# First layer's running states: sixteen chained products per sequence become seven single ones, added up in SBUF by GpSimd

## The chip, the cores and the metric

One core of one Trainium2 chip runs the whole program. The metric is the device time of one execution in microseconds; less is better. The kernel before was timed three times.

## What is computed

Four transformer layers follow each other on an input of 8 sequences of 512 tokens with 128 features. The change touches the attention of the first layer alone. Cut to what matters:

```python
def _L0_attn_ref(x, W1, b1, W2, b2):          # 16 heads of 8 features
    k, q, v = jnp.split(x @ W1 + b1, 3, axis=-1)
    mask = jnp.tril(jnp.ones((t, t), dtype=bool))
    attn = jnp.where(mask, jnp.einsum('bhqd,bhkd->bhqk', q, k), 0.0)
    out = jnp.einsum('bhqk,bhkd->bhqd', attn, v)
    return out @ W2 + b2
# x = x + _L0_attn_ref(_layernorm(x), ...), then a mixture of experts, then three more layers
```

There is no softmax, so the sum over earlier keys can be split. The 512 tokens are cut into 8 chunks of 64. Within a chunk the scores are made and masked. For all earlier chunks, q is multiplied with a state: the sum of k (outer) v over all tokens before the chunk, a 128x128 matrix of which the 16 diagonal blocks of 8x8 are kept. Chunks 1 to 7 need a state each.

## The kernel before

Each engine has its own program, and semaphores order them. For the first layer `STEPS0` gives every piece of work of a sequence b a due time on each engine that takes part, and `lanes` sorts the pieces of all 8 sequences by these times with 7.53 between sequences. The result, `ORDER0`, is one fixed list per engine. Each engine works its list strictly in order; a piece that waits holds up all behind it. The pieces are these: `l0a_s`/`l0a_n` are the normalisation (statistics on DVE, the inverse root by POOL's `rstd`, the scaling on DVE, transposes on PE, a copy by ACT), `l0_q` and `l0_kv` the projections, `l0_sc0` and `l0_sc1` the scores of chunks 0 to 3 and 4 to 7 with their masking on DVE, `l0_st` the states, `l0_o` the output, `l0_pj` the projection and the addition to X, `l0f_s`/`l0f_n` the second normalisation, and `l0t_*` the routing of the tokens. The last of these, `l0t_x`, is four indirect DMAs on POOL (line 2126).

I call the stretch from one `l0_st` to the next a step. In a middle step PE's list is (b is the sequence whose states are made)

    st.b  t_r.(b-2)  l0a_n.(b+2)  kv.(b+1)  sc0.(b+1)  o.b  t_c.(b-2)  l0f_n.(b-1)  pj.b  q.(b+2)  sc1.(b+1)

and DVE's is

    sc1.b  l0a_s.(b+3)  st.b  t_r.(b-2)  t_m.(b-2)  l0a_n.(b+3)  kv.(b+1)  sc0.(b+1)  l0f_n.(b-1)  t_w t_c t_i.(b-2)  pj.b  l0f_s.b

POOL's is `l0a_s.(b+3) l0a_n.(b+1) t_x.(b-3 or so) l0f_s.b`: for sequence 3, for instance, `t_x.0 f_s.2 a_s.6 a_n.4`.

`l0_st` on PE makes the seven states in one PSUM unit of two banks. State c (1 to 7) is the sum over the c // 2 whole tiles of 128 tokens before it, and half a tile (64 tokens) if c is odd. Each is summed in PSUM by a chain of products: 12 products over 128 rows (line 706) and 4 over 64 rows (line 708), 16 in all; whole and half products take turns. Every float32 product appears in the trace as two matrix instructions. DVE then multiplies the 896 columns by the head mask on their way to SBUF (line 1523, tile `l0_S`, which the trace calls K). `l0_o` waits for that and for the masked scores, then multiplies each state with q (line 738) and the scores with v (line 744). A ring of four PSUM units is shared by all pieces of the first layer (`unit`, `filled`, `drained`); a piece may fill its unit when the piece four units earlier has been drained.

Of the kernel before, what the change touches and what calls it, by code (L numbers as in the profile page):

```python
# [11 lines left out]
ALU = mybir.AluOpType  # L12
# [3 lines left out]
B, T, D, H, HD = 8, 512, 128, 16, 8  # L16
# [60 lines left out]
def lanes(pieces, gap):  # L77
# [18 lines left out]
    ("l0_st", dict(PE=21.86, DVE=22.8)),  # L96
# [240 lines left out]
def count_units():  # L337

    out, at, uses = {}, {3: 0, 4: 0}, [0] * 4
    for name, b in FILL:  # L340
        ring = 4 if name[:2] == "l0" else 3
        for k in range(UNITS.get(name, 0)):
# [13 lines left out]
         "logits_on", "hot", "tsub", "texp", "slots", "scatter0", "scatter1", "y0_in", "y1_in", "mixed",  # L356
# [8 lines left out]
def build(nc, inp, out):  # L365
    with ExitStack() as ctx:
# [99 lines left out]
        def drained_of(key, k=0):  # L466
            return drained[UNIT[key[0], key[1], k][0]]
# [20 lines left out]
        l0_S = [kflat[i][:, 512:1408].rearrange("p (c d) -> p c d", c=7) for i in range(2)]  # L488
        l0_oT = [tmpA[:, 1024 + 512 * i:1536 + 512 * i] for i in range(2)]
# [94 lines left out]
        def pe_program(e):  # L584
# [96 lines left out]
            for name, b in ORDER0["PE"]:  # L681
# [16 lines left out]
                elif name == "l0_st":  # L698
# [3 lines left out]
                    for c in range(1, 8):  # L702
                        t, half = divmod(c, 2)
                        o = p[:, 128 * (c - 1):128 * c]
                        for tt in range(t):
                            m = PE.matmul(o, ktok[i][:, tt, :], v_dense(i, tt, 0, 128), start=(tt == 0), stop=(tt == t - 1 and not half))
                        if half:
                            m = PE.matmul(o, ktok[i][0:64, t, :], v_dense(i, t, 0, 64), start=(t == 0), stop=True)
# [18 lines left out]
                elif name == "l0_o":  # L727
                    u, n, p = unit((name, b))
                    e.wait_ge(drained_of(("l0_st", b)), after(("l0_st", b)))
# [5 lines left out]
                    for t in range(4):  # L735
                        for c in range(2):
                            if 2 * t + c:
                                PE.matmul(p[:, 512 * c + 64 * t:512 * c + 64 * t + 64], l0_S[i][:, 2 * t + c - 1, :],
                                          qf[i][:, 128 * t + 64 * c:128 * t + 64 * c + 64], start=True, stop=False, skip_group_check=True)
# [374 lines left out]
        def dve_program(e):  # L1114
# [369 lines left out]
            for name, b in ORDER0["DVE"]:  # L1484
# [33 lines left out]
                elif name == "l0_st":  # L1518
                    u, n, p = unit((name, b))
                    if b > 1:  # L1520
# [3 lines left out]
                                    in0=p[:, 0:896].rearrange("p (c h e) -> p c h e", c=7, h=H),  # L1524
# [529 lines left out]
        def pool_program(e):  # L2054
# [81 lines left out]
            for name, b in ORDER0["POOL"]:  # L2136
                if name in ("l0a_s", "l0f_s"):
                    if (name, b) != ("l0a_s", 0):
                        rstd((name, b))
                elif name == "l0a_n":  # L2140
                    add_bias(("l0a_n", b), "l0_b2")
                elif name == "l0t_x":
                    scatter(0, b)
# [353 lines left out]
```

## Time and profile before

| what | value |
|---|---|
| time, median of 3 | 1372.38 us (1365.06, 1372.38, 1373.85) |
| span of the profiled execution | 1367.5 us |
| PE busy over the whole span | 1136.0 us, 83% |
| DVE busy | 824.0 us, 60% |
| ACT busy | 568.1 us, 42% |
| POOL busy | 447.1 us, 33% |
| the first layer's attention and routing | about 8 to 200 us of the span |

The span is the time from the first to the last instruction of one execution, and busy time is the time in which an engine has an instruction under way. A product on PE shows twice, as a weight load (PEld) and as the matrix pass (PE). The profiled execution is one of the faster: 4.9 us below the median.

### The profile page before, as it was taken

To read this page: it belongs to the slowest core of one execution; us is meant where nothing else is said; L and a number is where in the kernel's file an instruction comes from. 1 tells how busy PE (TensorE), PEld (TensorE's weight loads), DVE (VectorE), ACT (ScalarE), POOL (GpSimd) and SP (SyncE) were. 2 spreads that over 40 slices of the span, in tenths; PEclk is the share of its full clock that TensorE was granted. 3 is DMA by queue.
4 is the path that set the end of the run, shared out by engine and by line. 5 is a ranking of instruction groups with operands and counts; after the bars stand their busy time and mean duration, and the time that the engine had idled before them with its cause. 6 is when DMAs were issued, how large, how long until landed. Compare 5 with 4: busy or idle time off the path is not lost.

```text
span 1367.5 us, 39578 instructions
## 1 busy us (share of the span) xinstructions
PE 1136.0 (83%) x16979; PEld 814.2 (60%) x16979; DVE 824.0 (60%) x2399; ACT 568.1 (42%) x993; POOL 447.1 (33%) x538
## 2 busy tenths in 40 slices
PE   6999968888976798687888988888898887987895
PEld 4677747777764374444555655656565564654784
DVE  7587764568885122356858587686848675644432
ACT  3322102455452131314373754737375462542332
POOL 3123331344564144113122313233321302112575
PEclk9999979999986899899999999999999998999998
DMA  9355415533140421222211211212221110201784
GB/s 364 150 206 204 179 63 180 170 126 120 35 157 22 114 59 48 51 57 54 55 50 53 65 50 41 63 43 59 59 59 50 41 32 11 56 11 45 192 208 89
DMA packets 85169, 126.18 MB, mean 92 GB/s; under 512 B 14465, under 2 KB 66178, under 8 KB 84578
## 3 DMA queue, kind: packets, MB, share of 16 engines
q1 hardware_dynamic: 68258, 106.57, 24.6%
q0 software_dynamic: 10928, 13.64, 4.2%
q10 hardware_dynamic: 5808, 3.43, 1.0%
q8 instruction: 134, 2.20, 0.7%
q14 instruction: 41, 0.34, 0.1%
HBM read 50.92 MB, written 46.74 MB: 71 GB/s over the span
## 4 chain that ended last, share of the span: by engine, by line
PE 36%; DVE 25%; issue 16%; ACT 10%; POOL 6%; DMA 5%; SPq 2%; another core or an unknown queue 0%; ACTq 0%; DVEq 0%; POOLq 0%
DVE mx L1705 9%; ACT MW L1988 4%; DVE bst L1137 2%; PE ps L994 2%; PE ps L782 2%; PE ps L783 2%; DVE mx L1696 2%; PE ps L1058 2%; PE ps L795 1%; PE ps L985 1%; DVE X L1165 1%; POOL xs L2126 1%; PE ps L1089 1%; PE ps L907 1%; POOL rst L2072 1%
## 5 line engine op out<-in xcount | busy, mean ns | idle before, releaser
L1705 DVE TENSOR_REDUCE mx<-ps 128x2 f32<-128x1024 f32 (+3 forms) x176 | 188.7, 1121 | 30.2 <-PE ps L1026 30.0
L1988 ACT ACTIVATE MW<-ps 128x1024 f32<-128x1024 f32 x160 | 154.8, 1030 | 74.7 <-PE ps L1043 62.2
L2126 POOL DMA_INDIRECT xs<-xr,sidu x96 | 96.0, 1000 | 132.6 <-DVE sidu L1296 96.3
L2069 POOL TENSOR_SCALAR rst<-bmv 128x4 f32<-128x4 f32 x64 | 15.9, 248 | 288.0 <-DVE bmv L1140 287.4
L1058 PE MATMUL ps<-MW,Vp 128*16 128x128 f32 x2560 | 87.3, 277 | 4.7 <-ACT MW L1988 4.4
L1026 PE MATMUL ps<-K,Q 64*128 64x512 bf16 (+3 forms) x512 | 60.0, 303 | 18.7 <-DVE mx L1705 11.5
L1975 ACT ACTIVATE MW<-ps 128x1024 f32<-128x1024 f32 x64 | 63.4, 1027 | 27.5 <-PE ps L956 25.7
L1058 PEld LDWEIGHTS ps<-MW,Vp 128*16 128x16 f32 x2560 | 63.8, 97 | 16.1 <-ACT MW L1988 5.7
L2152 POOL DMA_INDIRECT out_dram<-qf,toku x39 | 60.7, 1555 | 35.3 <-DVE toku L1761 26.2
L1794 ACT COPY XT<-ps 128x512 f32<-128x512 f32 x48 | 28.2, 587 | 102.2 <-PE ps L616 85.7
L1696 DVE TENSOR_REDUCE mx<-ps 128x8 f32<-128x768 f32 x64 | 58.1, 950 | 16.6 <-PE ps L933 14.5
L1043 PE MATMUL ps<-Q,K 64*128 64x128 bf16 x1280 | 58.2, 221 | 5.6 <-DVE mx L1696 2.2
L2048 ACT ACTIVATE MW<-ps,MW 128x256 f32<-128x256 f32 (+1 forms) x92 | 34.0, 440 | 60.5 <-PE ps L1103 58.4
L616 PE MATMUL ps<-W,xr 128*128 128x128 f32 x192 | 33.8, 304 | 27.9 <-DVE xr L1150 16.5
L2152 POOL DMA_INDIRECT ys<-xp,toku x38 | 38.0, 1000 | 56.4 <-DVE toku L1549 47.6
L1137 DVE BATCH_NORM_STATS2 bst<-X 128x6 f32<-128x128 f32 x256 | 55.4, 279 | 1.2
L1043 PEld LDWEIGHTS ps<-Q,K 64*128 64x128 bf16 x1280 | 38.5, 95 | 27.3 <-issue 12.9
L2072 POOL TENSOR_TENSOR rst<-rst,npow 128x4 f32<-128x4 f32 x48 | 49.9, 1039 | 4.0
L782 PE MATMUL ps<-tco,MW 128*128 128x256 f32 x152 | 46.9, 391 | 3.7 <-ACT tco L1864 1.3
L1026 PEld LDWEIGHTS ps<-K,Q 64*128 64x128 bf16 x512 | 18.6, 94 | 50.9 <-DVE mx L1705 17.0
L649 PE MATMUL ps<-W,tmpA 128*128 128x128 f32 x256 | 40.5, 286 | 10.1 <-ACT MW L1988 4.1
L1165 DVE TENSOR_TENSOR X<-ps,X 128x512 f32<-128x512 f32 x40 | 27.6, 690 | 35.2 <-PE ps L754 11.5
(379 smaller groups left out, 2713.0 us busy)
## 6 DMA issues: line engine op xcount, KB each, us to landing
xs<-hb SPq DMA_DIRECT2D x52, 528.0 KB, 9.2
MW<-l_moe_dram SPq DMA_DIRECT2D x19, 768.0 KB
MW<-l_moe_dram SPq DMA_DIRECT2D x20, 578.0 KB
Q<-spl SPq DMA_DIRECT2D x48, 128.0 KB
Q<-spm SPq DMA_DIRECT2D x48, 128.0 KB
K<-spl SPq DMA_DIRECT2D x43, 128.0 KB
K<-spm SPq DMA_DIRECT2D x43, 128.0 KB
MW<-l_moe_dram SPq DMA_DIRECT2D x16, 256.0 KB
```

The costliest lines, as they stand in the source:

```text
L782: PE.matmul(p[:, 256 * jj:256 * jj + 256], wt_[:, 128 * j:128 * j + 128], xsT0[s % 2], start=True, stop=True)
L1026: m = PE.matmul(p[:, o:o + nk], Q3[i][64 * k:64 * k + 64, s, 128 * t:nk], K3[i][64 * k:64 * k + 64, s, 0:nk], start=True, stop=True, tile_ ...
L1043: m = PE.matmul(p[:, o:o + 128], K3[i][64 * k:64 * k + 64, 4 * half + s, 128 * kt:128 * kt + 128], Q3[i][64 * k:64 * k + 64, 4 * half + s, ...
L1058: m = PE.matmul(ps[32 * j:32 * j + 16, 7, 128 * g:128 * g + 128], Vp[1][:, 4 * i + kt, h, :], P3[k % 2][:, col(h)[0] + 128 * col(h)[1]:col ...
L1137: own.end(V.bn_stats(out=bst[:, k, t, :], in_=X[:, 4 * b + t, :]))
L1696: V.tensor_reduce(out=mx[0][:, :, 4 * half:4 * half + 4, t], in_=p.rearrange("p (e n) -> p e n", e=2)[:, :, 0:384].rearrange("p e (s k) -> ...
L1705: V.tensor_reduce(out=mx[1][:, :, s0:s0 + ns, t], in_=p.rearrange("p (e n) -> p e n", e=2)[:, :, 0:ns * nk].rearrange("p e (s k) -> p e s ...
L1975: A.activation(P2[t % 2][:, 1024 * half:1024 * half + 1024], p, ACT.Exp).then_inc(drained[u], 1)
L1988: A.activation(P3[k % 2][:, 1024 * half:1024 * half + 1024], p, ACT.Exp).then_inc(drained[u], 1)
L2072: G.tensor_tensor(out=rst[:, k, 1, :], in0=rst[:, k, 0, :], in1=npow[:, :], op=ALU.pow).then_inc(rstd_on[k], 1)
L2126: G.indirect_dma_start(out=xs[L], out_offset=bass.IndirectOffsetOnAxis(ap=sidu[:, 4 * b + t:4 * b + t + 1], axis=0), in_=src[:, t, :], in_ ...
L2152: G.indirect_dma_start(out=dst, out_offset=at, in_=y[:, v, :], in_offset=None, compute_op=how).then_inc(y_out[k], 16)
```

## The change

PE makes seven independent products per sequence: one for each of the three whole tiles and one for the first half of each of the four tiles. DVE masks them into SBUF as before. GpSimd (POOL) then adds: whole[1] += whole[0], whole[2] += whole[1], each 128x128, and half[1:4] += whole[0:3], 128x384; each addition waits for the one before. `l0_o` waits for a new semaphore, `states`, that the last addition raises, in place of DVE's drain. The tile holds the states in another order (three whole ones, then four odd ones), and `state_at` finds them. Since `l0_st` now has a due time of 33.0 on POOL, POOL's list becomes, for sequence 3, `t_x.0 f_s.2 st.3 a_s.6 a_n.4`: the additions stand before `l0a_s.(b+3)`.

```diff
-    ("l0_st", dict(PE=21.86, DVE=22.8)),
+    ("l0_st", dict(PE=21.86, DVE=22.8, POOL=33.0)),
...
+        def state_at(c):
+            return c // 2 - 1 if c % 2 == 0 else 3 + c // 2
...
-                    for c in range(1, 8):
-                        t, half = divmod(c, 2)
-                        o = p[:, 128 * (c - 1):128 * c]
-                        for tt in range(t):
-                            m = PE.matmul(o, ktok[i][:, tt, :], v_dense(i, tt, 0, 128), start=(tt == 0), stop=(tt == t - 1 and not half))
-                        if half:
-                            m = PE.matmul(o, ktok[i][0:64, t, :], v_dense(i, t, 0, 64), start=(t == 0), stop=True)
+                    for t in range(3):
+                        PE.matmul(p[:, 128 + 128 * t:256 + 128 * t], ktok[i][:, t, :], v_dense(i, t, 0, 128), start=True, stop=True)
+                    for t in range(4):
+                        m = PE.matmul(p[:, 512 + 128 * t:640 + 128 * t], ktok[i][0:64, t, :], v_dense(i, t, 0, 64), start=True, stop=True)
                     m.then_inc(filled[u], 1)
...
                 elif name == "l0_o":
-                    e.wait_ge(drained_of(("l0_st", b)), after(("l0_st", b)))
+                    e.wait_ge(sem["states"], b + 1)
...
-                                PE.matmul(..., l0_S[i][:, 2 * t + c - 1, :],
+                                PE.matmul(..., l0_S[i][:, state_at(2 * t + c), :],
...
-                                    in0=p[:, 0:896].rearrange("p (c h e) -> p c h e", c=7, h=H),
+                                    in0=p[:, 128:1024].rearrange("p (c h e) -> p c h e", c=7, h=H),
...
+                elif name == "l0_st":
+                    i, key = b % 2, ("l0_st", b)
+                    whole, half = l0_S[i][:, 0:3, :], l0_S[i][:, 3:7, :]
+                    e.wait_ge(drained_of(key), after(key))
+                    own.end(G.tensor_tensor(out=whole[:, 1, :], in0=whole[:, 1, :], in1=whole[:, 0, :], op=ALU.add))
+                    e.wait_ge(own.sem, own.now)
+                    own.end(G.tensor_tensor(out=whole[:, 2, :], in0=whole[:, 2, :], in1=whole[:, 1, :], op=ALU.add))
+                    e.wait_ge(own.sem, own.now)
+                    G.tensor_tensor(out=half[:, 1:4, :], in0=half[:, 1:4, :], in1=whole, op=ALU.add).then_inc(sem["states"], 1)
```

## Rows read from the trace of the kernel before

**Rows 1.** Busy time in a stretch: length, PE, PEld, DVE, ACT, POOL busy (xcount), PEclk, DMA, GB/s.
```profile
80.00:100.00 20.00, 19.48 (x409) 15.19 (x409) 15.73 (x58) 5.95 (x10) 7.77 (x9) 1.00 0.52 202
```

**Rows 2.** Timeline of PE, step 3: start us, us, what, xcount, idle before.
```profile
81.85 1.12 PE L722 MATMUL ps<-Q,K 32*64 32x256 f32 x32
82.90 0.49 PE L708 MATMUL ps<-Vp,tmpA 64*128 64x128 f32 x2
83.31 0.71 PE L706 MATMUL ps<-Vp,tmpA 128*128 128x128 f32 x4
83.95 0.48 PE L708 MATMUL ps<-Vp,tmpA 64*128 64x128 f32 x2
...
85.87 1.60 PE L706 MATMUL ps<-Vp,tmpA 128*128 128x128 f32 x12
87.41 0.49 PE L708 MATMUL ps<-Vp,tmpA 64*128 64x128 f32 x2
87.82 1.06 PE L631 MATMUL ps<-W,XT 128*128 128x12 f32 x8
...
92.08 0.43 PE L738 MATMUL ps<-qf,K 128*128 128x64 f32 x2
```

**Rows 3.** Timeline of DVE, step 3 and the next steps' first masks, same columns.
```profile
85.35 2.36 DVE L1516 TENSOR_TENSOR MW<-ps,W 128x1024 f32<-128x1024 f32 x2 [3.03 <-remote]
...
88.82 1.06 DVE L1523 TENSOR_TENSOR K<-ps,W 128x896 f32<-128x896 f32 x1
...
90.57 0.87 DVE L1188 TENSOR_TENSOR spm<-spm 128x16 f32<-128x16 f32 x1
...
91.98 1.11 DVE L1150 TENSOR_SCALAR xr<-X,bmv,rst 128x128 f32<-128x128 f32 x4
...
96.66 1.10 DVE L1150 TENSOR_SCALAR xr<-X,bmv,rst 128x128 f32<-128x128 f32 x4
...
101.25 0.69 DVE L1165 TENSOR_TENSOR X<-ps,X 128x512 f32<-128x512 f32 x1
...
105.87 1.23 DVE L1516 TENSOR_TENSOR MW<-ps,W 128x1024 f32<-128x1024 f32 x1 [2.61 <-remote]
...
126.01 2.36 DVE L1516 TENSOR_TENSOR MW<-ps,W 128x1024 f32<-128x1024 f32 x2 [1.91 <-remote]
...
146.75 2.36 DVE L1516 TENSOR_TENSOR MW<-ps,W 128x1024 f32<-128x1024 f32 x2 [3.93 <-remote]
...
163.73 2.36 DVE L1516 TENSOR_TENSOR MW<-ps,W 128x1024 f32<-128x1024 f32 x2 [1.06 <-remote]
```

**Rows 4.** Timeline of DVE, steps 1 and 2, same columns.
```profile
43.79 2.36 DVE L1516 TENSOR_TENSOR MW<-ps,W 128x1024 f32<-128x1024 f32 x2 [1.34 <-PE ps L722]
...
63.00 2.36 DVE L1516 TENSOR_TENSOR MW<-ps,W 128x1024 f32<-128x1024 f32 x2 [0.72 <-PE ps L722]
```

**Rows 5.** Timeline of POOL, step 3, same columns.
```profile
80.37 1.23 POOL L2126 DMA_INDIRECT xs<-xr,sidu  x1 [11.32 <-DVE sidu L1296]
...
84.45 0.96 POOL L2126 DMA_INDIRECT xs<-xr,sidu  x1 [0.30 <-issue]
...
89.31 1.04 POOL L2072 TENSOR_TENSOR rst<-rst,npow 128x4 f32<-128x4 f32 x1
90.32 1.09 POOL L2083 TENSOR_TENSOR X<-X,W 128x512 f32<-128x512 f32 x1
```

**Rows 6.** POOL's instructions grouped by line and form: xcount, busy us, mean ns.
```profile
L2189 POOL TENSOR_TENSOR rr<-rr,rt 128x512 f32<-128x512 f32 x16 | 20.5, 1279 | 75.4 <-DVE rt L1661 75.4
L2113 POOL TENSOR_TENSOR mx<-mx,msp 128x64 f32<-128x64 f32 x16 | 4.9, 308 | 1.3
```

**Rows 7.** Busy time in a stretch at half clock and the one before it, columns as in Rows 1.
```profile
34.60:38.00 3.40, 1.89 (x98) 1.41 (x85) 0.00 (x0) 0.38 (x1) 0.00 (x0) 1.00 0.03 9
38.00:41.40 3.40, 3.14 (x10) 2.54 (x11) 0.93 (x3) 0.20 (x1) 0.00 (x0) 0.50 0.46 188
```

**Rows 8.** Timeline of PE at the end of the states, last sequence.
```profile
167.96 0.43 PE L738 MATMUL ps<-qf,K 128*128 128x64 f32 x2 [0.44 <-DVE K L1523]
```

More of the change, by code:

```diff
@@ L355 @@
          "pv0", "pv1", "og_out0", "og_out1",
-         "logits_on", "hot", "tsub", "texp", "slots", "scatter0", "scatter1", "y0_in", "y1_in", "mixed",
+         "logits_on", "hot", "states", "tsub", "texp", "slots", "scatter0", "scatter1", "y0_in", "y1_in", "mixed",
          "tab", "pattern", "g_half", "gx0", "gx1", "gx2", "gx3", "gw0", "gw1", "gw2", "gw3", "turned", "gT", "g_act", "g_down", "g_y", "g_tok",
@@ L737, in pe_program @@
                             if 2 * t + c:
-                                PE.matmul(p[:, 512 * c + 64 * t:512 * c + 64 * t + 64], l0_S[i][:, 2 * t + c - 1, :],
+                                PE.matmul(p[:, 512 * c + 64 * t:512 * c + 64 * t + 64], l0_S[i][:, state_at(2 * t + c), :],
                                           qf[i][:, 128 * t + 64 * c:128 * t + 64 * c + 64], start=True, stop=False, skip_group_check=True)
```

## Prediction

> **What bounds the kernel now.** I first looked for the place of the change in the timeline of PE. The states of sequence 3 take PE from 82.90 to 87.82, 4.92 us, and the row below each run shows where it ends [rows 2]. The busy time per stretch then says whether PE is what the first layer waits for: 19.48 of 20 us busy at full clock, DVE 15.73, POOL 7.77 [rows 1]. PE is the bound of this stage, and time taken from it should be time won, eight times. That is the tempting answer. The rest of the reading asks what comes second, and how far behind.
>
> For that I followed one step on DVE and POOL. X is the moment at which PE's last score product of a step ends, s the moment at which DVE starts the first mask of these scores. In step 3, X is 81.85 + 1.12 = 82.97 [rows 2] and s is 85.35 [rows 3]: DVE had waited 3.03 us, and the trace has no instruction as the releaser ("remote"). In steps 1 and 2, s (43.79 and 63.00) comes 0.1 us after the product [rows 4]. What is new from step 3 on is POOL's series of four indirect DMAs, 80.37 to 85.41 [rows 5]; all five steps that have it show the wait [rows 3]. So a mask signal seems to arrive 2 to 3 us late while POOL issues these DMAs. I take this as it stands; the cause is not in the rows.
>
> From s, DVE runs without a gap that matters: masks and statistics to the state mask at 88.82 = s + 3.5, its end at s + 4.5, routing, scaling of sequence b+3 at 91.98 = s + 6.6, the second norm's scaling at 96.66 = s + 11.3, the addition to X at 101.25 = s + 15.9 and statistics to s + 17.9 [rows 3]. A step takes 20.5 us (85.35 to 105.87). DVE is thus only 2.6 us behind PE, less than what the change takes from PE.
>
> **What PE gives up.** A run of 12 instructions lasts 85.87 to 87.41, 1.54 us, one of 4 lasts 83.31 to 83.95, 0.64 us [rows 2]: 0.11 us an instruction and 0.20 us for each turn between whole and half products. Before: 32 x 0.11 + 7 x 0.20 = 4.92, as the trace has it. After: 7 products are 14 instructions, 1.54 us, and 2 turns, 0.40: 1.95 us. PE gives up 3.0 us per sequence, 24 us in all.
>
> **What POOL adds.** The trace has no addition of this size on POOL. Below lies 128x64 at 308 ns, above 128x512 at 1279 ns [rows 6] or 1090 ns [rows 5]. On the line through 308 and 1090 (1.75 ns a column) 128 columns take 0.42 and 384 take 0.87 us: 2 x 0.42 + 0.87 + three handovers of 0.07 to 0.1 = 1.95 us, which I round to 2.0 with the first wait. The ends are 3 x 0.31 = 0.9 and 3 x 1.28 = 3.8 us. I take the line, since both sizes lie inside it.
>
> POOL's own page bears on this. The Trainium skill (GPSIMD Engine Reference, section 3.1) gives an addition on GpSimd about 2.6 cycles per element at 1.2 GHz. By that estimate 640 columns would be 1.4 us plus dispatch; the rows and the page agree within what the ends leave open.
>
> Then I place the additions. They need DVE's state mask, whose end is s + 4.55, so the states are ready at s + 6.65, where the old `l0_o` needed only s + 4.55. In steps 0 to 4 the inverse root for sequence b+3 (1.04 us [rows 5] and 0.3 for the short instruction before it, 1.35 us) now queues behind them on POOL: ready at s + 8.0 where it was ready at s + 5.0. DVE needs it at s + 6.6 and stands 1.4 us; everything behind it on DVE (kv, score masks, second norm) moves by that. The second norm's scaling ends at s + 13.8, and PE's transposes wait for it. Where no sequence b+3 exists (steps 5 to 7) this does not arise.
>
> One more thing is shared. The routing addition of 128x16 on DVE took 0.87 us at 90.57 [rows 3], while POOL's big addition ran from 90.32 to 91.41 [rows 5]; it ended with it. So DVE operations with two SBUF inputs stand still while POOL adds. Three such operations follow the state mask. In steps 3 and 4 they fall into the 1.4 us that DVE loses anyway; in steps 5 and 6 they may cost DVE up to 1 us, which is covered, since PE needs the norm only at s + 11.5 and DVE has it at s + 10.2.
>
> The Trainium skill states this as a rule (SBUF — State Buffer, section "SBUF: two separate sides"): the port pair of VectorE and GpSimd is an exclusive lock. It speaks against work on GpSimd; here it would add at most 2 steps x 1 us if the cover were gone, 2 us to the sum.
>
> **Step by step.** Old PE from X to `l0_o`: 92.08 - 82.97 = 9.1 us, 8.2 in steps 0 and 1, which have no routing product (0.9) [rows 2].
>
> - Step 0: PE could start `l0_o` at X + 5.3, the states come at X + 0.1 + 6.7 = X + 6.8. Gain 1.5, and PE stands 1.5.
> - Step 1: `l0_o` at s + 6.7, its end s + 12.3 (5.6 us without the fetch gap in it), norm at s + 13.8, then transposes, projection, q and scores 0.5 + 0.9 + 1.8 + 1.05: X' = s + 18.2. It was 19.2 (43.79 to 63.00 [rows 4]): gain 0.9.
> - Step 2 likewise, then the late signal (2.4 to 3 us): 20.8 against 22.35 (63.00 to 85.35): 1.5.
> - Steps 3 and 4: X' = s + 18.1, DVE ready at s + 19.3, signal at s + 20.8, against 20.5 and 20.1 [rows 3]: lost 0.3 and 0.7. DVE starts POOL's next DMAs at s + 17.4, so X' again falls inside them.
> - Step 5: no b+3. States at s + 5.4, X' = s + 16.2, signal s + 19.3, against 20.7: gain 1.4. Step 6, without q: X' = s + 13.95 and signal s + 16.1, against 17.0: gain 0.9.
> - Step 7: the states come at s + 5.5, PE started `l0_o` at 167.96 = s + 4.2 [rows 8]: lost 1.2.
>
> Sum: 1.5 + 0.9 + 1.5 - 0.3 - 0.7 + 1.4 + 0.9 - 1.2 = 4.0 us gained out of 24. The rest of PE's 24 us turns into standing before `l0_o` and before the second norm, some 3 us per step.
>
> **The clock.** The granted clock was 0.50 from 38.0 to 41.4, that is the level of 1.2 GHz, after PE had been busy for only 1.89 of the 3.40 us before [rows 7], and such a stretch costs half its length, 1.7 us. New standing of 1.5 us twice a step invites more of them. I allow one more than before: 4.0 - 1.7 = 2.3 us. The profiled span of 1367.5 becomes 1365.2. The median of the runs stands 4.9 us above that span, so I predict 1370.1 us. Later stages get the same instructions in the same order and I move nothing there.
>
> **The rivals.**
>
> A. PE's time counts in full: 24 us, 1348 us. For it speaks the 97% of PE [rows 1]. It needs states at X + 6.2, while even with s = X + 0.1 they come at X + 6.8. Chance 0.06.
>
> B. The signal is no longer late, because X' and the DMAs part. Then steps 2 to 6 run at DVE's s + 19.3 or PE's X': up to 1.5 to 2 us more each, 8 us in all: 1362 us. Chance 0.12.
>
> C. POOL's additions cost as much as its dearest row, 1.28 us each [rows 6]. 3.84 us in place of 1.95, 1.9 us more in each of 8 steps, 15 us: 1385 us, slower. It passes the old time once the three additions exceed 1.95 + 2.3 / 8 = 2.2 us, and is slower by 1% from about 4 us. Against it, a quarter of the columns at a quarter of the row's price is the pattern of the rows. Chance 0.10.
>
> D. The clock drops in every step: 8 x 1.7 = 13.6 in place of 1.7, so 1382 us. For it speaks standing of 3 us per step; against it, PE has about 1 us of cover in steps 1 to 4. Chance 0.10. The Trainium skill (TensorE: Matmul & The Clock Gate, Part 1) says that idle time returns PE to the half rate; the trace agrees at 38.0.
>
> My own case holds 0.62.
>
> **How the numbers follow.** A measurement of this kernel can tell about 1%, 13.7 us, from no change. The range runs from B's 1362 less 3 for the spread of the runs (1365 to 1374) up to D's 1382: 1359 to 1382 us. It leaves out A (0.06) and most of C (0.10). A lies below 1358.7, and of B a few hundredths may; above 1386.1 lie half of C, by the spread of the runs, and little of D. Faster 0.08, same 0.84, slower 0.08.
>
> **What would show it.** PE's states take 1.95 us (14 instructions). POOL shows three additions of about 0.42, 0.42 and 0.87 us per sequence. PE stands 1.5 us before line 738 with POOL as the releaser, and before line 616 with DVE's scaling. DVE's line 1150 waits about 1.4 us for POOL's inverse root in steps 0 to 4. PE's busy time falls by 24 us, the span hardly. The end of the first layer comes 2 to 4 us earlier. I am wrong if the additions are far from 2 us, if s is no longer 2 to 3 us behind X, or if stretches at 1.2 GHz appear in most steps.

## The result, and the profile after

| kernel | median | runs | ratio to before, 95% interval | profiled span |
|---|---|---|---|---|
| before | 1372.43 us (1365.06 to 1375.33) | 15 | | 1367.5 us |
| after | 1382.31 us (1373.72 to 1391.70) | 15 | 1.0072 [1.0051, 1.0094] | 1375.3 us |

The change makes the kernel 0.7% slower: less than 1%, but clear of zero, and to the other side of the small gain I had worked out. The predicted 1370.1 us is 12 us too low, and 1382.3 lies just above the range. The same text gave 1.0040 [1.0018, 1.0062], 1.0039 [1.0013, 1.0065] and 1.0072 [1.0046, 1.0097] in three further comparisons, each on another chip.

The first layer's end can be read in both traces, from the mark that POOL sets after the last indirect DMA. The first line is before, timeline of POOL (start, us, what):

```profile
199.40 0.10 POOL L2062 MEMSET mark<- 128x1 f32 x1 [1.42 <-DMA xs<-xr,sidu]
```

and this is after, same view:

```profile
209.58 0.10 POOL L2064 MEMSET mark<- 128x1 f32 x1 [1.44 <-DMA xs<-xr,sidu]
```

So the first layer ends 10.2 us later, and the span grows by 7.8; the rest of the program took 2.4 us less in this execution. All that follows is about these 10.2 us. With s as in the prediction (start of DVE's first mask of a step), the steps of both kernels in us are:

| step | 0 | 1 | 2 | 3 | 4 | 5 | 6 | last s to the mark |
|---|---|---|---|---|---|---|---|---|
| before | 21.0 | 19.2 | 22.3 | 20.5 | 20.1 | 20.7 | 17.0 | 35.7 |
| after | 21.4 | 20.8 | 22.8 | 21.3 | 21.3 | 20.6 | 17.5 | 40.8 |
| predicted change | -1.5 | -0.9 | -1.5 | +0.3 | +0.7 | -1.4 | -0.9 | +1.2 |
| measured change | +0.4 | +1.5 | +0.4 | +0.8 | +1.2 | -0.1 | +0.5 | +5.1 |

(The first s is 0.3 us later as well.) Every step misses by 0.5 to 2.4 us, the tail by 3.9.

After, timeline of PE, step 3; it answers to [rows 2]. The field in brackets is the idle time before the row and what ended it:

```profile
85.84 0.94 PE L708 MATMUL ps<-Vp,tmpA 128*128 128x128 f32 x6
86.71 1.16 PE L710 MATMUL ps<-Vp,tmpA 64*128 64x128 f32 x8
88.89 1.06 PE L636 MATMUL ps<-W,XT 128*128 128x12 f32 x8 [1.03 <-ACT K L1847]
89.81 0.63 PE L621 MATMUL ps<-W,xr 128*128 128x128 f32 x4
90.41 3.37 PE L701 MATMUL ps<-W,XT 128*128 128x256 f32 x8
...
95.00 0.43 PE L740 MATMUL ps<-qf,K 128*128 128x64 f32 x2
...
102.75 0.63 PE L621 MATMUL ps<-W,xr 128*128 128x128 f32 x4 [1.12 <-DVE xr L1152]
```

The states take 85.84 to 87.87, 2.0 us, as worked out. But two things follow that the sum did not have. PE stands 1.03 us for ACT's copy of q (it holds the PSUM unit that the next piece wants; before, the 4.92 us of products covered it). And the k and v products of line 701 take 3.37 us, in a stretch of half clock (1.89 us in e8_gap_fill below, at the full one).

After, timeline of DVE, step 3; it answers to [rows 3]:

```profile
88.00 2.35 DVE L1518 TENSOR_TENSOR MW<-ps,W 128x1024 f32<-128x1024 f32 x2 [2.71 <-remote]
...
91.47 1.06 DVE L1525 TENSOR_TENSOR K<-ps,W 128x896 f32<-128x896 f32 x1
...
96.12 1.80 DVE L1152 TENSOR_SCALAR xr<-X,bmv,rst 128x128 f32<-128x128 f32 x4 [1.39 <-POOL rst L2074]
...
101.50 1.10 DVE L1152 TENSOR_SCALAR xr<-X,bmv,rst 128x128 f32<-128x128 f32 x4
...
109.30 1.22 DVE L1518 TENSOR_TENSOR MW<-ps,W 128x1024 f32<-128x1024 f32 x1 [1.22 <-remote]
```

After, timeline of POOL, step 3; it answers to [rows 5]:

```profile
89.09 1.05 POOL L2074 TENSOR_TENSOR rst<-rst,npow 128x4 f32<-128x4 f32 x1
92.61 0.46 POOL L2148 TENSOR_TENSOR K<-K 128x128 f32<-128x128 f32 x1 [2.47 <-DVE K L1525]
93.14 0.45 POOL L2150 TENSOR_TENSOR K<-K 128x128 f32<-128x128 f32 x1
93.67 1.02 POOL L2152 TENSOR_TENSOR K<-K 128x384 f32<-128x384 f32 x1
94.67 0.22 POOL L2071 TENSOR_SCALAR rst<-bmv 128x4 f32<-128x4 f32 x1
94.97 1.04 POOL L2074 TENSOR_TENSOR rst<-rst,npow 128x4 f32<-128x4 f32 x1
95.98 1.09 POOL L2085 TENSOR_TENSOR X<-X,W 128x512 f32<-128x512 f32 x1
```

The three additions take 92.61 to 94.69, 2.1 us. The inverse root waits behind them and is ready at 96.01 = s + 8.0, and DVE stands 1.39 us for it: all of this as predicted. New is the length of DVE's scaling at 96.12. It takes 1.80 us where [rows 3] has 1.11, because POOL's addition of the bias (95.98 to 97.07) now runs beside it. In the kernel before, that addition met the small routing operation instead (0.87 us in [rows 3]). Now that operation takes 0.40 us beside POOL's first additions, and a later one (line 1196) 0.66 us, both within the time that DVE loses anyway. The second norm is therefore ready at 102.60 = s + 14.6, not s + 13.8.

After, busy time in stretches, columns as in [rows 1], to be laid beside [rows 1] and [rows 7]:

```profile
60.10:63.50 3.40, 3.40 (x10) 1.78 (x8) 1.94 (x9) 0.32 (x1) 0.22 (x1) 0.51 0.78 318
172.80:206.90 34.10, 23.29 (x320) 18.70 (x321) 20.82 (x119) 2.48 (x6) 14.50 (x16) 0.50 0.06 21
80.00:100.00 20.00, 18.21 (x319) 13.27 (x320) 14.74 (x57) 5.35 (x9) 9.65 (x12) 0.83 0.45 179
```

The granted clock is at the level of 1.2 GHz once in every step (36.3 for 6.8 us, then 60.1, 80.6, 90.9, 111.3, 131.8 and 152.3 for 3.4 us each), where before had it at 38.0 only. At the end it stays there for 34.1 us (before 17.1, from 178.0). In the stretch 80 to 100 PE is busy for 18.21 us in place of 19.48, at a mean clock of 0.83 in place of 1.00. Over the whole span it is busy for 1129.3 us in place of 1136.0: 6.7 us less and not 24, while its mean granted clock falls from 0.946 to 0.931. The prediction's last sign of being wrong, stretches at 1.2 GHz in most steps, is there.

After, timeline of PE in the last sequence; it answers to [rows 8]:

```profile
175.10 0.69 PE L740 MATMUL ps<-qf,K 128*128 128x64 f32 x2 [5.55 <-POOL K L2152]
175.72 1.19 PE L746 MATMUL ps<-MW,Vp 64*32 64x64 f32 x64
176.84 1.11 PE L740 MATMUL ps<-qf,K 128*128 128x64 f32 x4
```

PE stands 5.55 us where it stood 0.44, and then works at half the clock (1.11 us for four instructions, 0.66 at the full one).

### The profile page after: what moved, and what is told of

Its sections match the earlier page's. It is cut to its first block, busy times and chain, and to the rows that moved or that the text cites. A ratio compares the mean times of both kernels' runs of the same rounds, so it can differ in the third digit from the quotient of the medians.

```text
span 1375.3 us, 39322 instructions
## 1 busy us (share of the span) xinstructions
PE 1129.3 (82%) x16835; PEld 809.6 (59%) x16835; DVE 829.9 (60%) x2399; ACT 567.6 (41%) x993; POOL 461.6 (34%) x562
## 3 DMA queue, kind: packets, MB, share of 16 engines
q1 hardware_dynamic: 68258, 106.57, 24.4%
## 4 chain that ended last, share of the span: by engine, by line
PE 36%; DVE 27%; issue 14%; ACT 9%; POOL 5%; DMA 4%; SPq 1%; another core or an unknown queue 1%; PEldq 1%; ACTq 0%; DVEq 0%; PEld 0%; POOLq 0%
DVE mx L1707 9%; ACT MW L1990 4%; DVE bst L1139 2%; PE ps L996 2%; DVE MW L1518 2%; PE ps L1105 2%; PE ps L1091 2%; PE ps L784 2%; PE ps L1060 2%; PE ps L785 1%; PE ps L797 1%; PE ps L987 1%; DVE X L1167 1%; DVE mx L1698 1%; DVE xr L1152 1%
## 5 line engine op out<-in xcount | busy, mean ns | idle before, releaser
L1028 PE MATMUL ps<-K,Q 64*128 64x512 bf16 (+3 forms) x512 | 60.5, 305 | 17.8 <-DVE mx L1707 10.3
L1698 DVE TENSOR_REDUCE mx<-ps 128x8 f32<-128x768 f32 x64 | 58.0, 949 | 16.7 <-PE ps L935 14.6
L1152 DVE TENSOR_SCALAR xr<-X,bmv,rst 128x128 f32<-128x128 f32 x128 | 39.6, 370 | 29.4 <-POOL rst L2074 27.8
L621 PEld LDWEIGHTS ps<-W,xr 128*128 128x128 f32 x192 | 24.2, 159 | 43.3 <-issue 20.6
L654 PE MATMUL ps<-W,tmpA 128*128 128x128 f32 x256 | 40.4, 285 | 10.2 <-ACT MW L1990 4.1
```

The lines of the kernel that those rows point to most:

```text
L621: m = PE.transpose(p[:, 128 * t:128 * t + 128], xr_of(key)[:, t, 0:128], ident)
L1028: m = PE.matmul(p[:, o:o + nk], Q3[i][64 * k:64 * k + 64, s, 128 * t:nk], K3[i][64 * k:64 * k + 64, s, 0:nk], start=True, stop=True, tile_ ...
L1698: V.tensor_reduce(out=mx[0][:, :, 4 * half:4 * half + 4, t], in_=p.rearrange("p (e n) -> p e n", e=2)[:, :, 0:384].rearrange("p e (s k) -> ...
```

## The experiments

The theories before the first run: **order** (the inverse root behind the additions on POOL delays DVE, and PE's second norm with it), **clock** (the half-clock stretches cost what their length says), **tail** (the last sequence alone), **additions** (their 2 us are on the path), and as their rival that **PE's relief** is worth something which something else eats. Steps are given as in the table above. "Before" beside a run is the kernel before on the same chip.

### Undoing one part each

**e1_no_additions**: the seven products without the additions (the states are then incomplete); `l0_o` waits for DVE's drain.

```diff
-                    e.wait_ge(sem["states"], b + 1)
+                    e.wait_ge(drained_of(("l0_st", b)), after(("l0_st", b)))
```

> The changed kernel with the three GpSimd additions left out (the later chunks' states are then incomplete); the output products wait for DVE's mask as before. This is what the shorter product work is worth when the sum is free. Theory 1 (the way over GpSimd is what costs: additions of 2 us before the output products, the inverse root behind them): the states are there at s + 4.6 instead of s + 6.6, no wait of DVE for the inverse root, a step of 18 to 18.5 us in place of 20.5 to 22.8, some 2 us won per step against the kernel before: 1355 to 1360 us. Theory 2 (PE's saved time can't be used at all, since DVE and the ring of PSUM units bind anyway): 1368 to 1374 us, no difference from before.

Measured: 0.9963 [0.9945, 0.9982] (before 1360.37). First layer's end 191.0 us. PE's relief alone is worth 0.37%, 5 us, of the 24 us that PE gives up. (Later stages work on other values here, since the states lack terms; that their time is unaffected by this is not shown.)

**e2_root_first**: the kernel after with one number changed, so that POOL's list is `t_x f_s a_s st a_n`, the inverse root ahead of the additions.

```diff
-    ("l0_st", dict(PE=21.86, DVE=22.8, POOL=33.0)),
+    ("l0_st", dict(PE=21.86, DVE=22.8, POOL=33.5)),
```

> The changed kernel with the due time of the additions on POOL at 33.5 in place of 33.0, so that the inverse root of sequence b+3 stands before the additions in POOL's list; everything else is the same. Theory 1a (the inverse root behind the additions is the larger part of the loss, by DVE and then by PE's transposes): DVE's waits for it (3.6, 3.6, 1.4, 1.4, 1.4 us) vanish, steps 1 to 4 are 1 to 1.5 us shorter: 1375 us. Theory 3 (the clock: PE's standing before the transposes is what lets it fall to 1.2 GHz in each step) expects in addition fewer half-clock stretches between 50 and 115 us, and 1370 to 1372 us. If neither holds the time stays at 1382.

Measured: 0.9998 [0.9973, 1.0022]. Steps 18.6 17.3 18.9 19.4 19.2 19.7 18.6, then 41.2, mark 196.2. The number undoes the loss, but gains nothing on the kernel before. Its median, 1358.49 us, is 3.4 us above e1's on the same chip: that is what the additions still cost with the root ahead of them.

**e7_additions_only**: the kernel before with its sixteen products, and three additions of the same sizes on POOL (`z` is a spare tile), whose results nobody needs; `l0_o` waits for them.

```diff
+                elif name == "l0_st":
+                    ...
+                    own.end(G.tensor_tensor(out=z[:, 0:128], in0=l0_S[i][:, 1, :], in1=l0_S[i][:, 0, :], op=ALU.add))
+                    ...
+                    G.tensor_tensor(out=z[:, 256:640], in0=kflat[i][:, 640:1024], in1=kflat[i][:, 1024:1408], op=ALU.add).then_inc(sem["states"], 1)
```

> The kernel before, with all its 16 products, but with three GpSimd additions of the same sizes into a spare tile, at the same place in GpSimd's list, and the output products waiting for them. It has the whole cost of the change and none of its relief. Where mask signals are in time, s = X + 0.1, the additions end at X + 6.8 and the output products start at X + 9.1 anyway, the norm is ready at X + 14.6 against 15.6: no loss but for the last sequence, 1.000 to 1.002. Where they are 2 to 3 us late the additions end at X + 9.3 and the norm is 1.5 us late: 1 to 2 us a step from step 3 on, 1.004 to 1.008. By the clock theory it is 1.000 on either chip, since PE hardly stands.

Measured: 1.0081 [1.0050, 1.0111] (before 1359.69); first layer's end 208.3. The additions with their wait cost 0.8%; with e1 (on another chip) that closes within the intervals: -0.4% for PE's relief, +0.8% for the additions, and +0.4% is what the kernel after shows on e7's chip. I had expected 1.000 to 1.002 for a chip without late mask signals, and this is one: that miss says that the cost needs no late signal. One view of e7, groups of DVE's instructions by line (the last field is the idle time before them and what ended it), shows where the cost enters, even with PE's old list:

```profile
L1150 DVE TENSOR_SCALAR xr<-X,bmv,rst 128x128 f32<-128x128 f32 x52 | 17.8, 401 | 13.2 <-POOL rst L2072 13.2
```

The same group before (on another chip; b1_before_trace and e4_before_grouped wait for the root as long, 3.2 us):

```profile
L1150 DVE TENSOR_SCALAR xr<-X,bmv,rst 128x128 f32<-128x128 f32 x52 | 14.4, 341 | 3.2 <-POOL rst L2072 3.2
```

DVE waits 10 us more for the inverse root and is 3.4 us longer busy with the scaling. (Both views run from 20 to 215 us. The 3.2 us of before lie after the last sequence's states; inside the steps it waits for no root, and e7 11.3 us: 3.57 in steps 0 and 1, 1.39 in each of 2 to 4.)

**e5_dve_additions**: the additions on DVE, right behind its mask; POOL's list as before.

> The changed kernel's seven products, with the three additions on DVE right behind its mask, and GpSimd's list as before the change. Theory 1 (what costs is the way over GpSimd): three DVE additions of about 0.3, 0.3 and 0.6 us with handovers, 1.3 us in place of 2.05, and no inverse root behind them: the states at s + 5.9, the norm on PE 1.3 us later than in the kernel before, 0.998 to 1.002 of it. Theory 2 (DVE is the next bound, so any time given to DVE is lost): DVE's own step grows to 19.2 us, and with PE at 17 to 18 the ratio is still 0.995 to 1.000. Above 1.003 both would be wrong.

Measured: 1.0018 [0.9990, 1.0046] (before 1369.66); steps 21.1 16.8 19.1 23.2 23.3 21.9 16.7, then 40.6. Its step 1, 16.8 us, is shorter than that of any other kernel that computes all the states; but the tail is as long as in the kernel after. So a long tail does not need POOL to do the additions; how much of it the wait for them makes is measured by e10 and e11 below.

### The kernel after, before and root-first on other chips

Here **a1_after_again**, **a2_after_third** and **a3_after_fourth** are the kernel after, **b0_before_again** and **b1_before_trace** the kernel before, **e2b_root_first** is e2's text.

> The kernel before, unchanged, on the chip of this group of runs, for its trace. The other chip's trace had mask signals 2 to 3 us late while GpSimd issued its DMAs; the traces of e1_no_additions to e4_before_grouped have none. If the lateness belongs to the chip or the execution and not to the kernel, it is absent here too, and a middle step takes 20.1 us by PE alone, as there; if it belongs to the length of the state products it is back.

> The changed kernel, unchanged, beside the others. e2_root_first came out at 0.9998 of the kernel before with one change of order; if the inverse root behind the additions is the cause of the loss, this one is again at 1.006 to 1.009. If it comes out at 1.000 too, the loss belonged to the first chip (late signals, clock), and the order has no part in it.

> The changed kernel, unchanged, for comparison with the other order on one chip: 1.004 to 1.007 of the kernel before, as on the two chips so far.

> The edit of e2_root_first again, now on the same chip as the changed kernel. If the inverse root behind the additions carries the loss, this stays at 1.000 +/- 0.002 while the changed kernel is at 1.004 or above. If the difference between the two was that of the chips, both have the same ratio.

> The kernel before, for a trace on the same chip as the other three. 1.000. If the late mask signals belong to the chip, all four kernels of this call show them or none does; if they belong to the kernel's timing, they may differ. The first layer's end without late signals is expected at 192 to 197 us, with them at 199 to 202 us.

> The kernel after once more, on the chip of e11. 1.004 to 1.007 as on the three chips before; tail 39 to 41.2 us, PE's stand in front of the last l0_o 4.8 to 5.6 us, clock at half from 166-173 us on for 34 us or in several stretches of as much together. Step 1 (no late signal on any chip) 20.7 to 20.8 us.

| label | ratio, 95% interval | steps | last s to the mark | mark |
|---|---|---|---|---|
| b0_before_again | 0.9989 [0.9965, 1.0014] | 19.0 19.3 22.4 21.4 20.5 20.1 17.9 | 37.8 | 201.5 |
| b1_before_trace | 1.0030 [1.0002, 1.0057] | 19.3 19.3 22.4 20.5 20.1 19.2 17.9 | 35.4 | 197.2 |
| a1_after_again | 1.0040 [1.0018, 1.0062] | 20.4 20.7 20.6 22.9 22.6 20.3 16.9 | 39.2 | 206.7 |
| a2_after_third | 1.0039 [1.0013, 1.0065] | 21.7 20.8 20.0 20.3 20.1 18.6 18.6 | 41.2 | 204.4 |
| a3_after_fourth | 1.0072 [1.0046, 1.0097] | 20.5 20.7 20.6 23.0 23.0 21.8 17.5 | 40.8 | 210.7 |
| e2b_root_first | 0.9995 [0.9969, 1.0021] | 18.6 17.3 19.2 19.2 19.3 18.0 18.6 | 41.2 | 194.6 |

The kernel before came out at 1.0030 against itself once. Differences of 0.3% between single comparisons are therefore not evidence; four comparisons of the kernel after, all above 1.0035, are. The mark is the sharper measure: 206.7 to 210.7 us (204.4 on a2's chip) against 197.2 to 201.5. On a2's chip, which has no late mask signals, the kernel before has no trace; what is compared with a2 there is e2b, 9.8 us earlier.

Step 1 repeats best, since no mask signal is late in it: 19.2 or 19.3 us in three traces of before, 20.7 or 20.8 in four of after, 17.3 in three of root-first (e2, e2b and, below, e10). Its rows show the order theory at work. DVE in step 1 of b1_before_trace:

```profile
42.38 2.36 DVE L1516 TENSOR_TENSOR MW<-ps,W 128x1024 f32<-128x1024 f32 x2 [0.72 <-PE ps L722]
47.27 1.09 DVE L1523 TENSOR_TENSOR K<-ps,W 128x896 f32<-128x896 f32 x1 [1.34 <-PE ps L708]
48.28 1.11 DVE L1150 TENSOR_SCALAR xr<-X,bmv,rst 128x128 f32<-128x128 f32 x4
...
53.25 1.11 DVE L1150 TENSOR_SCALAR xr<-X,bmv,rst 128x128 f32<-128x128 f32 x4
```

in a2_after_third:

```profile
44.76 2.36 DVE L1518 TENSOR_TENSOR MW<-ps,W 128x1024 f32<-128x1024 f32 x2 [2.38 <-PE ps L724]
48.23 1.05 DVE L1525 TENSOR_TENSOR K<-ps,W 128x896 f32<-128x896 f32 x1
52.85 1.81 DVE L1152 TENSOR_SCALAR xr<-X,bmv,rst 128x128 f32<-128x128 f32 x4 [3.57 <-POOL rst L2074]
...
58.24 1.09 DVE L1152 TENSOR_SCALAR xr<-X,bmv,rst 128x128 f32<-128x128 f32 x4
```

and in e2b_root_first:

```profile
41.69 2.36 DVE L1518 TENSOR_TENSOR MW<-ps,W 128x1024 f32<-128x1024 f32 x2 [0.73 <-PE ps L724]
45.15 1.06 DVE L1525 TENSOR_TENSOR K<-ps,W 128x896 f32<-128x896 f32 x1
46.78 3.06 DVE L1152 TENSOR_SCALAR xr<-X,bmv,rst 128x128 f32<-128x128 f32 x4 [0.57 <-POOL rst L2074]
...
53.42 1.10 DVE L1152 TENSOR_SCALAR xr<-X,bmv,rst 128x128 f32<-128x128 f32 x4
```

The second norm is ready at s + 12.0 before, s + 14.6 after, s + 12.8 with the root first. In steps 0 and 1 there is no routing work to fill the gap, so DVE stands 3.57 us for the root, not 1.4; I had read the wait off step 3. With the root first the wait is 0.57 us, but the scaling takes 3.06 us in place of 1.11. It now runs beside the additions themselves and the bias, timeline of POOL in e2b_root_first:

```profile
46.65 0.45 POOL L2148 TENSOR_TENSOR K<-K 128x128 f32<-128x128 f32 x1
47.18 0.46 POOL L2150 TENSOR_TENSOR K<-K 128x128 f32<-128x128 f32 x1
47.72 0.99 POOL L2152 TENSOR_TENSOR K<-K 128x384 f32<-128x384 f32 x1
48.67 1.09 POOL L2085 TENSOR_TENSOR X<-X,W 128x512 f32<-128x512 f32 x1
```

Part of what the order gives is lost again in the longer scaling.

The comparison of the two orders by one number was made on two chips without late mask signals only. On chips with them the root-first order ran with other edits: e10 came out at 1.0018 and its counterpart with the root behind the additions, e11, at 1.0053, each on its own chip.

### The clock inside the steps

**e3_fill**: the kernel after with dummy products of 512 columns wherever PE stands (two before `l0_o`, two before `l0f_n`, one before `l0a_n`).

> The changed kernel with dummy products on PE, written to the unused half of a unit, where PE would stand: two before the output products, two before the transposes of the second norm, one before those of the first from sequence 2 on (0.86 us each at full clock). They do nothing but keep PE busy. Theory 3 (half of the loss and more is the clock): the stretches at 0.50 between 43 and 165 us vanish or become few, and the last one begins later than 172.8 us; the dummies themselves cost about 1 us a step where PE was not standing; net 1372 to 1378 us. Theory 1 (only the chain over GpSimd and DVE costs, the clock is a companion): 1382 us or up to 8 us slower, for the dummies' own time.

Measured: 1.0183 [1.0148, 1.0217]. The dummies were too long for the gaps (a pair takes 1.98 us); PE then works without a gap from 79.8 to 88.0, and steps 2 to 5 take 22.2 to 23.9 us. The half-clock stretches are gone in steps 0 to 2, where PE's clock is full until 89.8, and stand once in each of steps 3 to 6. With so much work added the time says nothing on what the clock costs.

**e8_gap_fill**: the same idea, smaller. Four dummies of 128 columns stand at the head of the states, where PE waits for ACT anyway, and one before `l0f_n` of sequences 0 to 3.

```diff
+                    for _ in range(4):
+                        PE.matmul(p[:, 0:128], ident, W[:, 0:128], start=True, stop=True)
```

> The changed kernel with four dummy products of 128x128 ahead of the state products (0.88 us, written to a part of the PSUM unit that nobody reads) and one of 128x512 ahead of the transposes of the second norm of sequences 0 to 3 (0.86 us). The first fall before a wait of 1.03 us for ACT, the second into a wait of 1.1 to 2.2 us for DVE, so that they delay nothing (DVE takes up the states 1.5 us after PE has made them). Clock theory: the half-clock stretches in the steps become fewer and the kernel 2 to 6 us faster than the changed one. Chain theory (the waits themselves cost, the clock follows and costs little, since PE waits anyway): the same as the changed kernel, within 2 us.

Measured: 1.0037 [1.0014, 1.0061], beside 1.0039 for the kernel after on the same chip. The stretches at 1.2 GHz between steps 1 and 6 are all gone. Steps 21.4 19.0 20.0 20.3 20.1 18.6 17.3, then 41.2; mark 200.9. Against a2_after_third that is 0.3 us less in step 0, 1.8 in step 1, 1.3 in step 6, and nothing in steps 2 to 5 although two clock stretches (88, 129) went from them. In step 1 DVE's rows are those of the kernel after to 0.1 us (wait 3.57 us, norm ready at s + 14.6), and what changed is PE after it, timeline of PE in e8_gap_fill:

```profile
60.40 1.02 PE L695 MATMUL ps<-XT,W 128*128 128x512 f32 x2
61.26 1.02 PE L696 MATMUL ps<-XT,W 128*128 128x512 f32 x2
```

against a2_after_third:

```profile
61.12 1.91 PE L694 MATMUL ps<-XT,W 128*128 128x512 f32 x2
62.82 1.58 PE L695 MATMUL ps<-XT,W 128*128 128x512 f32 x2
```

So a half-clock stretch costs 1.3 to 1.8 us where it falls on q or the last products of a step, and nothing where it falls on line 701 while PE would soon have stood anyway. All in all the clock inside the steps is worth 3.5 us of the mark here, on a chip on which the kernel after has five such stretches; the other traces of it have seven or eight. The 3.5 us are not in the time: e8's median is 0.9 us above a2's. That is within what a ratio can tell (its interval is 6 us wide), but it leaves the clock's price in the whole time open.

**e9_root_first_fill**: e8's four dummies in the root-first kernel.

> Root first on POOL as in e2_root_first, plus four dummy products of 128 columns at the head of each sequence's states (0.9 us of PE's work that the kernel doesn't need). Clock theory (the half-clock stretches inside the steps cost what their length says): they vanish as in e8_gap_fill, the sum over the steps falls by 3 to 5 us against e2_root_first and the ratio is 0.996 to 0.997. Chain theory (they are companions of PE's standing and cost nothing): same step lengths as e2_root_first within 0.5 us each, ratio 0.999 to 1.001.

Measured: 1.0102 [1.0073, 1.0131] (before 1370.39), steps 21.9 17.8 18.8 24.6 20.8 21.7 16.3, then 41.5, mark 206.3. Neither theory had this. The half clock came back in another place (91 us, 10.2 us long, and again at 142), so there the dummies did not hold the clock. The dummies' own time can't be the reason where it can be read: in step 2 the piece behind the states starts 3.06 us after the score products, as in e8, and 3.05 us in a2 without dummies, where PE waits for ACT. Mask signals are late on this chip (3.8 us of waiting before step 6 alone) and e9 has the old 41.5 us of tail; what makes the rest of the loss, and why the median lies 9 us above e10's while the marks differ by 5.7, stays open.

### The tail

**e10_root_first_old_last** and **e11_after_old_last**: the root-first kernel and the kernel after, with the last sequence alone as in the kernel before: sixteen products, `l0_o` behind DVE's mask, no additions.

```diff
-                    e.wait_ge(sem["states"], b + 1)
+                    if b == B - 1:
+                        e.wait_ge(drained_of(("l0_st", b)), after(("l0_st", b)))
+                    else:
+                        e.wait_ge(sem["states"], b + 1)
...
```

> The seven products with the inverse root ahead of the additions on POOL, as in e2_root_first, but for the last sequence the kernel before's sixteen chained products, its mask and its wait: no additions there. Theory (what is left of the loss after the order is mended is the tail: PE stands 4.8 us in front of the last output piece, and the clock stays at half for 34 us there): PE's stand in front of l0_o of the last sequence falls to about 0.4 us, the stretch from the last sequence's first score mask to the end of the first layer from 41.2 to 36-37 us, the first layer ends 4 to 5 us earlier than in the root-first kernel and the ratio to before is 0.9995 - 0.0035 = 0.996 (0.994 to 0.998). Rival (the half clock in the tail comes from the routing and the switch to the next stage, not from the stand): the half-clock stretch keeps its 34 us, the tail its 41 us and the ratio stays at 1.000. Second rival (the end of the first layer is not what the next stage waits for): the tail shortens and the ratio stays at 1.000.

> The kernel after, its list on POOL included, but for the last sequence the kernel before's sixteen products, mask and wait. Theory (the tail is one of the two parts of the loss, for its stand and the clock that falls with it): in front of the last l0_o PE stands 0.4 us in place of 4.8 to 5.6; the stretch from the last first mask to the end of the first layer is 36 to 38.5 us in place of 39 to 41; the first layer ends 2.5 to 4.5 us earlier than in the kernel after on this chip, and the ratio to before is 0.002 to 0.003 lower. Rival (what the first layer's end gains is given back later, the end being followed by a stage that waits for transfers): the first layer ends earlier by that much and the ratio stays within 0.001.

Measured: e10 1.0018 [0.9993, 1.0042], steps 20.5 17.3 19.4 23.6 20.7 20.8 17.2, tail 38.3 (e9 on the same chip 41.5), mark 200.6 (b1, the kernel before on this chip, 197.2). e11 1.0053 [1.0034, 1.0073], steps 20.7 20.7 20.0 24.4 22.7 20.6 17.2, tail 38.2 (a3 on the same chip 40.8), mark 207.5 (a3 210.7). PE's stand is gone, as the timeline of e11 shows:

```profile
173.46 0.43 PE L751 MATMUL ps<-qf,K 128*128 128x64 f32 x2 [0.44 <-DVE K L1536]
...
174.62 1.11 PE L751 MATMUL ps<-qf,K 128*128 128x64 f32 x4
```

but the clock falls all the same, 1.2 us after the first of these rows (3.4 us later than in a3), and stays down for 27.3 us in sum. The tail is worth 2.5 to 3.2 us of the mark. In the ratio it is 0.0019 (e11 against a3), less than two such comparisons can tell apart, and the 0.996 that I expected of e10 did not come; how much of the tail reaches the whole time is not shown. The clock drop in the tail needs no stand of 5 us; b0_before_again has one of 27.3 us too, with a tail of 37.8.

### PE's own time

**e4_before_grouped**, **e4b_grouped** and **e4c_grouped**: the kernel before with its sixteen products in another order, the twelve whole ones first, so that PE turns twice and not seven times (counted as in the prediction, with the turn into the first run). In e4 each sum was started by its own product, and the states then lack the whole tiles; e4b (and e4c, the same text) set the start flag only on the first product into each bank, and all seven states are complete.

> The kernel before with its 16 chained products in another order: first the 12 over 128 rows, then the 4 over 64 rows, so that the kinds take turns twice instead of eight times; no GpSimd, no other change. By the 0.20 us per turn read from the rows, PE's states take 3.9 us in place of 4.9: with PE as the bound 1.0 us won in each of 8 steps, 1364 us, and no more half-clock stretches than before. If PE is not the bound of a step in the kernel before, nothing: 1372 us.

> As e4_before_grouped (16 chained products, the 12 whole ones first, then the 4 half ones), but only the first product into each of the two PSUM banks starts a sum; in e4_before_grouped every sum was started by its own product, and the half products then no longer added to the whole ones, so its states lacked the whole tiles. The instructions and their times are the same: 0.996 to 0.999 of the kernel before, 3.8 us of PE for the states in place of 4.9, its gain of 1.1 us a step visible in the steps if PE is the bound there.

> The kernel before with its sixteen products in another order, the twelve whole ones first, then the four half ones, nothing else: the same text as e4b_grouped. PE's states take 3.95 us in place of 4.9. If PE's millisecond share in each step counts, 8 x 0.95 = 7.6 us at most, 0.9945; if only steps in which DVE's signal isn't late profit, 0.998 (0.996 to 1.000), as on the two chips before.

Measured: 0.9978 [0.9956, 0.9999], 0.9989 [0.9967, 1.0012] and 1.0004 [0.9984, 1.0025]. (The "millisecond share" in the last expectation is a slip: PE's share in microseconds.) The states take 3.95 us in place of 4.92, as 0.20 us per turn says, 7.8 us over eight sequences, and by the ratios the time changes by -3.0, -1.5 and +0.5 us (the first with e4's incomplete states). PE's time was hardly on the path even before the change.

No version that computes everything beat the kernel before by more than the measurement can tell.

## Why the prediction was wrong, point by point

**Right.** PE as the apparent bound and DVE 2.6 us behind; the products 4.92 to 2.0 us; the additions 0.46, 0.45 and 1.02 with their handovers 2.1 us (predicted 1.95, rival C's 3.8 excluded); states at s + 6.7 in steps 0 to 4, root at s + 8.0; DVE's wait of 1.39 us in steps 2 to 4; A's 24 us not to be had: e1, with no additions at all, gained 5. The late mask signals stayed where POOL's DMAs are, so B did not come on this chip. The 4.9 us that I had set between the profiled span and the median were 7.0 here (1375.3 and 1382.3), so 2.1 us of the 12 are in that term.

**Wrong, the clock's "one more than before".** This was rival D, which I gave 0.10. Seven stretches came in place of one in the steps. I had read the one row of a drop and the 3 us of new standing, and discounted it by "about 1 us of cover". The price of 1.7 us each was about right where PE was on the path (1.3 to 1.8 us in steps 1 and 6 by e8), and zero elsewhere, so D's 13.6 us looks too much as well: e8 puts five stretches at 3.5 us of the mark. That the measured time fell on D's 1382 is luck: several terms made it, not the clock alone.

**Wrong, "norm at s + 13.8" in steps 0 to 4.** It was s + 14.6. I had seen that POOL's bias addition holds up a DVE operation (0.87 us in [rows 3]) and let that end, but had not asked which operation the addition meets after the move. It meets the scaling, 1.80 in place of 1.11 us, on the path. I had also counted only DVE operations with two SBUF inputs as held up; the scaling reads one tensor, and the rows show it held up (1.11 us alone, 1.80 beside the bias, 3.06 beside the additions and the bias). The Trainium skill (SBUF — State Buffer, section "SBUF: two separate sides") has the pair of ports that VectorE and GpSimd share as an exclusive lock, held for a whole instruction, and names two kinds of VectorE operation that take it: those with two SBUF inputs and those in a 2-port mode. The rows agree with such a lock; whether the scaling runs in a 2-port mode no run shows.

**Wrong, the wait for the root in steps 0 and 1.** I worked with 1.4 us from step 3's rows. Without the routing work DVE has nothing before the scaling, and stands 3.56 us. The norm is ready no later for it, so this alone did not move the sum (whose four terms for step 1 give s + 18.05, not 18.2, too little to matter); but it is why root-first gains most there (20.8 to 17.3 in step 1: 1.7 us from the norm, 1.8 from the clock by e8).

**Missed, the wait for ACT.** PE stands 1.03 us after the states in each of steps 0 to 6, for a PSUM unit that ACT frees (the trace names ACT in four of them, in a2 in all seven). Of the 3.0 us that PE gives up 2.0 are left where PE is the bound. In step 5 the states did not decide, as I had it (s + 5.4): `l0_o` started at 137.22 = s + 6.6, at the end of PE's own line, which had lost 1.03 us to ACT and some 1.7 us to the clock.

**Wrong, the tail's 1.2 us.** It is 5.1: the last `l0_o` starts at s + 6.3, 2.1 us later than before, the length of the additions. I had it at s + 5.5; DVE's state mask starts at s + 3.0 as before, since it waits 0.66 us for a late signal where the shorter products should have let it start earlier. Then `l0_o` takes 8.2 us in place of 5.6, at half the clock, 2.6 us more. e10 and e11 take 2.5 to 3.2 us of it back.

Sum of the causes in the mark, as far as the runs show them: the first layer was to end 4.0 us earlier (2.3 with the clock) and ended 10.2 later. The tail accounts for 3.9 of the 14.2 us, the clock in the steps for 3.5 (measured on another chip), the longer scaling for up to 0.8 in each of steps 1 to 4. The rest, some 4 us, has the wait for ACT in it, up to 1 us in each step in which PE is the bound, and is not split further. The cause of the loss itself is cleaner than that sum: e2's one number turns 1.0039 into 0.9995 on the same chip, 1364.65 us into 1358.70, with the mark at 194.6 in place of 204.4.

## What to carry to other kernels

When work leaves the busiest engine, first time the chain through the other engines without it: here e4 and e1 say that 8 and 24 us less on PE are worth 0 to 5. When work is put on another engine's list, the price is not its length but what queues behind it and which instruction of the port's other user it now runs beside; put it behind what others wait for (here one due time, 33.0 or 33.5, decided between a loss of 0.4% and none). And a stand that is new, short and once per step is to be counted as a possible half-clock stretch per step (here five to eight in place of none or one), to be paid where the bound engine works next.

## What the runs showed of the hardware

**Late signals go with the chip, not with the kernel.** In 12 of the 20 traces, those of the first comparison and of three later ones, DVE's masks wait 8.5 to 13.4 us in sum for a releaser that the trace doesn't have, from step 2 or 3 on, and the first mask of such a step starts 1.6 to 3.5 us after the last score product, while POOL issues its indirect DMAs (it is 0.1 us in steps 1 and 2, [rows 4]). In the other 8, from two chips, there is none of it. Each chip was used in one comparison only, so chip and occasion can't be told apart. Groups of DVE's instructions by line, a3_after_fourth:

```profile
L1518 DVE TENSOR_TENSOR MW<-ps,W 128x1024 f32<-128x1024 f32 x32 | 37.8, 1217 | 15.0 <-remote 10.7 <-PE ps L724 4.3
```

and a2_after_third, the same text on another chip:

```profile
L1518 DVE TENSOR_TENSOR MW<-ps,W 128x1024 f32<-128x1024 f32 x32 | 37.4, 1209 | 5.9 <-PE ps L724 5.9
```

In a2_after_third the product ends at 105.38 and the mask starts at 105.84, in the midst of four indirect DMAs (104.28 to 109.18). The two quiet chips also have the two lowest medians of the kernel before, 1359.69 and 1360.37 us against 1369.66 to 1372.43. What differs between the chips no run shows.

**A small addition on GpSimd** takes 0.45 us for 128x128 and 1.00 to 1.02 for 128x384 in float32: 2.15 ns a column and 0.18 us of its own. That line also gives 0.32 us for 64 columns and 1.28 us for 512, as [rows 6] has them (308 and 1279 ns). The bias addition's 1.09 us, from which I had drawn my line, lies below it, and so my 0.87 us for 384 columns was short by 0.15 us. By the Trainium skill (GPSIMD Engine Reference, section 3.1), about 2.6 cycles an element at 1.2 GHz, an estimate of the slope is 2.17 ns; the trace agrees.
